# Attention and squared-ReLU block on one core: the turned pair of heads leaves for DRAM whole and returns in strips, and the opening loads x and w_proj in another order

## The reference, cut to what matters

```
xn  = layernorm(x)
qkv = xn @ Wqkv + bqkv                       # 16 heads of 32
attention over blocks of 128 tokens: a block sees itself and its two neighbours,
    masked to |kpos - qpos| <= 128, softmax(scores / sqrt(512))
a   = attn @ values, heads joined, @ Wout + bout
w(W)= ternary(W) * row scale                 # scale = mean |W| of a row
h   = xn @ w(w_fc).T + gate * (xn @ v.T @ fast_b.T @ u.T)
f   = max(h, 0)^2 @ w(w_proj).T
out = x + a + f
```

## Time and profile before

| | us |
|---|---|
| median of 3 runs | 2447.55 (2446.18 to 2448.85) |
| the profiled execution | 2450.27 |
| its span, first to last instruction | 2448.5 |
| TensorE busy | 2355.4 (96%) |
| VectorE busy | 1678.4 (69%) |
| ScalarE busy | 1378.8 (56%) |
| GpSimd busy | 440.5 (18%) |

### The profile page before, as it was taken

The page is one execution under the profiler, slowest core; times in us unless marked ns, Lnnn a source line. Parts: engine busy times, 40 slices in busy tenths (PEclk is TensorE's granted clock), DMA queues, the critical chain, the costliest instruction groups (busy, mean ns, idle before and its releaser), DMA issues.

```text
span 2448.5 us, 56233 instructions
## 1 busy us (share of the span) xinstructions
PE 2355.4 (96%) x19528; PEld 1919.7 (78%) x19528; DVE 1678.4 (69%) x4576; ACT 1378.8 (56%) x3488; POOL 440.5 (18%) x734
## 2 busy tenths in 40 slices
PE   6999999999999999988999999999999999999996
PEld 5788888888888888867787777777777878888785
DVE  5455545555554454436888888888888888888885
ACT  6333333333333333325777677777777777777774
POOL 2011111111111111002222222222222222222221
PEclk8999999999999999999999999999999999999998
DMA  4733344433334444315999999999999999999995
GB/s 158 218 110 106 104 119 120 120 107 107 111 105 118 120 120 120 94 43 160 267 291 278 272 287 281 288 280 288 283 280 287 290 278 287 290 290 283 287 279 174
DMA packets 437149, 495.74 MB, mean 202 GB/s; under 512 B 35728, under 2 KB 359824, under 8 KB 436416
## 3 DMA queue, kind: packets, MB, share of 16 engines
q1 hardware_dynamic: 436784, 492.71, 68.0%
q0 software_dynamic: 144, 0.17, 0.0%
HBM read 261.53 MB, written 231.21 MB: 201 GB/s over the span
## 4 chain that ended last, share of the span: by engine, by line
PE 13%; DMA 12%; ACT 9%; issue 7%; DVE 7%; SPq 6%; POOL 0%; POOLq 0%; DVEq 0%
ACT wqkv_raw L1124 6%; DMA wqkv_raw<-turned_blocks 5%; DMA pair_moved<-turned_pairs 5%; DVE wqkv_raw L1202 4%; PE job_ps L1503 4%; SPq L1015 3%; SPq L1007 3%; PE job_ps L1343 3%; PE score_ps L1430 3%; PE job_ps L1352 2%; ACT pT L1133 2%; DMA turned_pairs<-pair_blocks 1%; DVE pair_blocks L1229 1%; ACT k_hi L1152 1%; ACT q_hi L1149 1%
## 5 line engine op out<-in xcount | busy, mean ns | idle before, releaser
L1124 ACT ACTIVATE wqkv_raw<-wqkv_raw,neg_max 128x384 f32<-128x384 f32 (+1 forms) x1024 | 621.6, 608 | 223.1 <-DVE neg_max L1202 221.0
L637 ACT ACTIVATE relu<-up_ps,fc_scale 128x512 f32<-128x512 f32 x256 | 176.7, 690 | 632.7 <-PE up_ps L747 632.7
L1202 DVE CUSTOM_DVE_ANT_0 wqkv_raw<-score_ps,mask 128x384 f32<-128x384 f32 (+1 forms) x1024 | 504.1, 549 | 29.1 <-PE score_ps L1430 28.8
L698 DVE SCALAR_TENSOR_TENSOR sq<-up_ps,relu 128x512 f32<-128x512 f32 x256 | 177.2, 692 | 493.0 <-ACT relu L637 491.8
L757 PE MATMUL down_ps<-proj_T,sq_hi 128*128 128x512 f32 x1024 | 404.4, 395 | 1.5 <-DVE sq_lo L681 1.5
L759 PE MATMUL down_ps<-proj_T,sq_lo 128*128 128x512 f32 x1024 | 404.7, 395 | 0.0
L743 PE MATMUL up_ps<-f_xT_hi,fc_T 128*128 128x512 f32 x1024 | 399.4, 390 | 2.2 <-PEq L136 2.2
L745 PE MATMUL up_ps<-f_xT_lo,fc_T 128*128 128x512 f32 x1024 | 399.5, 390 | 0.0
L1219 DVE STREAM_TRANSPOSE wqkv_raw<-wqkv_raw 128x384 f32<-128x384 f32 (+1 forms) x508 | 283.5, 573 | 68.9 <-ACT wqkv_raw L1124 65.9
L1343 PE MATMUL job_ps<-xT_hi,wqkv_hi 128*128 128x256 f32 x1024 | 310.5, 303 | 0.1
L1343 PE MATMUL job_ps<-xT_lo,wqkv_hi 128*128 128x256 f32 x1024 | 289.5, 283 | 0.0
(11 more groups left out here) (158 smaller groups left out, 4391.2 us busy)
## 6 DMA issues: line engine op xcount, KB each, us to landing
turned_blocks<-wqkv_raw SPq DMA_DIRECT2D x123, 768.0 KB, 5.5
wqkv_raw<-turned_blocks SPq DMA_DIRECT2D x492, 192.0 KB, 3.9
turned_pairs<-pair_blocks SPq DMA_DIRECT2D x496, 96.0 KB, 2.7
pair_moved<-turned_pairs SPq DMA_DIRECT2D x124, 384.0 KB, 4.9
xT_hi<-xT SPq DMA_DIRECT2D x65, 256.0 KB, 5.8
xT_lo<-xT SPq DMA_DIRECT2D x65, 256.0 KB, 5.6
xT<-f_xT_hi SPq DMA_DIRECT2D x64, 256.0 KB, 2.9
xT<-f_xT_lo SPq DMA_DIRECT2D x64, 256.0 KB, 3.0
```

The source lines that it names most:

```text
L637: nc.scalar.activation(relu[:, s % 2, :], up_ps[:, s % 2, :], ACT.Relu, scale=fc_scale2[:, s:s + 1]).then_inc(relu_done, 1)
L698: nc.vector.scalar_tensor_tensor(sq[:, s % 2, :], up_ps[:, s % 2, :], 0.0, relu[:, s % 2, :], ALU.max, ALU.mult).then_inc(sq_done, 1)
L1124: nc.scalar.activation(probs[:, u, cols], probs[:, u, cols], ACT.Exp, bias=neg_max[:, u:u + 1], scale=-1.0, accum_out=prob_sum[:, u:u + 1] ...
L1202: nc.vector.tensor_tensor_reduce(out=probs[:, u, cols], in0=score_ps[:, h, cols], in1=mask[:, cols], scale=-SCORE_SCALE, scalar=3e38, op0= ...
```

## The change

The pair's transfers change shape. On the way out, the whole of `pair_blocks` goes in one transfer over 128 partitions; for the last token pair, where only two of three neighbours are seen, too. DRAM now holds it as [128 partitions][4 strips][3][64], so that a partition's part is one contiguous run of 3072 bytes where it was four of 768. On the way in, four transfers each fetch one strip into 32 partitions of `pair_moved`, as the blocks have done all along. The waits on `pair_out` and `pair_in` follow in number.

In the opening, the four blocks of x are issued one behind each of `w_fc` blocks 7 to 10, `w_proj` goes in halves of 512 KB: four of them behind `w_fc` blocks 12 to 15, four behind the last. VectorE does the low parts of x at its steps 16, 17, 18 and 19 in place of 14, 15, 17 and 18.

```diff
-        X_LOW_AT = (FB - 2, FB - 1, FB + 1, FB + 2)
+        X_LOW_AT = (FB, FB + 1, FB + 2, FB + 3)
...
+            def load_proj(piece):
+                k, half = divmod(piece, 2)
+                cols = slice(half * F // 2, (half + 1) * F // 2)
+                sp.dma_start(proj_rows[k][:, cols], w_proj[k * P:(k + 1) * P, cols]).then_inc(proj_here[k], 16)
...
-                if n == BUFS - 1:
-                    for b, here in enumerate(lead.x_here):
-                        sp.dma_start(lead.x_in[:, b, :], block_rows(x, b)).then_inc(here, 16)
-                if n >= FB - DC:
-                    k = n - FB + DC
-                    sp.dma_start(proj_rows[k], w_proj[k * P:(k + 1) * P, :]).then_inc(proj_here[k], 16)
+                if BUFS - 1 <= n < BUFS - 1 + DC:
+                    b = n - BUFS + 1
+                    sp.dma_start(lead.x_in[:, b, :], block_rows(x, b)).then_inc(lead.x_here[b], 16)
+                elif n >= FB - DC:
+                    load_proj(n - FB + DC)
+            for piece in range(DC, 2 * DC):
+                load_proj(piece)
...
-                for q in range(STRIPS):
-                    sp.dma_start(pair_dram[t % 2, q, :, :, 0:last, :].rearrange("a j w x -> j a (w x)"),
-                                 pair_blocks[q * DH:(q + 1) * DH, :, 0:last, :, :].rearrange("j a w h t -> j a (w h t)")
-                                 ).then_inc(pair_out, 16)
+                if last == 3:
+                    sp.dma_start(pair_dram[t % 2, :, :, :, :].rearrange("p a w x -> p (a w x)"),
+                                 pair_blocks.rearrange("p a w h t -> p (a w h t)")).then_inc(pair_out, 16)
...
-                sp.wait_ge(pair_out, 16 * STRIPS * (t + 1))
+                sp.wait_ge(pair_out, 16 * (t + 1))
                 if t >= 1:
                     sp.wait_ge(pv_done, t)
-                sp.dma_start(pair_moved[:, :, 0:last, :, :].rearrange("p q w h t -> p q (w h t)"),
-                             pair_dram[t % 2, :, :, :, 0:last, :].rearrange("q a j w x -> (a j) q (w x)")).then_inc(pair_in, 16)
+                for a in range(STRIPS):
+                    moved = pair_dram[t % 2, :, a, 0:last, :].rearrange("(q j) w x -> j q (w x)", j=DH)
+                    sp.dma_start(pair_moved[a * DH:(a + 1) * DH, :, 0:last, :, :].rearrange("j q w h t -> j q (w h t)"),
+                                 moved).then_inc(pair_in, 16)
...
-    pair_dram = nc.dram_tensor("turned_pairs", [2, P // DH, P // DH, DH, 3, 2 * DH], F32, kind="Internal").ap()
+    pair_dram = nc.dram_tensor("turned_pairs", [2, P, P // DH, 3, 2 * DH], F32, kind="Internal").ap()
```

More of the change, by code:

```diff
@@ L236, in sum_proj @@
             def sum_proj(n):
-                dve.wait_ge(proj_here[n], 16)
+                dve.wait_ge(proj_here[n], 32)
                 nc.vector.tensor_reduce(abs_sum[:, FB + n:FB + n + 1], rows(FB + n), AX_X, ALU.add,
@@ L402, in sum_abs @@
                 else:
-                    act.wait_ge(proj_here[n - FB], 16)
+                    act.wait_ge(proj_here[n - FB], 32)
                     w = proj_rows[n - FB]
@@ L1013, in move_pair_out @@
                 sp.wait_ge(pair_turned, MOVED * (t + 1))
-                for q in range(STRIPS):
-                    sp.dma_start(pair_dram[t % 2, q, :, :, 0:last, :].rearrange("a j w x -> j a (w x)"),
-                                 pair_blocks[q * DH:(q + 1) * DH, :, 0:last, :, :].rearrange("j a w h t -> j a (w h t)")
-                                 ).then_inc(pair_out, 16)
+                if last == 3:
+                    sp.dma_start(pair_dram[t % 2, :, :, :, :].rearrange("p a w x -> p (a w x)"),
+                                 pair_blocks.rearrange("p a w h t -> p (a w h t)")).then_inc(pair_out, 16)
+                else:
+                    sp.dma_start(pair_dram[t % 2, :, :, 0:last, :].rearrange("p a w x -> p a (w x)"),
+                                 pair_blocks[:, :, 0:last, :, :].rearrange("p a w h t -> p a (w h t)")).then_inc(pair_out, 16)
             def move_pair_in(t):
@@ L1227, in turn_pair @@
                 if h == 0 and t >= 1:
-                    dve.wait_ge(pair_out, 16 * STRIPS * t)
+                    dve.wait_ge(pair_out, 16 * t)
                 nc.vector.transpose(pair_blocks[:, :, seen.start:seen.stop, h, :].rearrange("p a w t -> p w a t"),
@@ L1487, in probs_times_values @@
                     if b == 1 and is_moved(t):
-                        pe.wait_ge(pair_in, 16 * (t + 1))
+                        pe.wait_ge(pair_in, 16 * STRIPS * (t + 1))
                     seen = blocks_seen(i, b)
```

## The result

| | before | changed |
|---|---|---|
| median, us (4 runs each) | 2446.86 (2444.58 to 2448.85) | 2404.36 (2401.08 to 2407.63) |
| the profiled execution, its span | 2450.27, 2448.5 | 2402.34, 2400.5 |
| start of the first up product | 59.42 | 52.22 |
| start of the first score product | 1124.66 | 1118.54 |
| mean step, 115 steps in mid attention | 10.207 | 9.935 |

The ratio is 0.9827, 95% interval 0.9808 to 0.9845: 42.5 us faster, where 38 were forecast. The two profiled executions differ by 47.9 us. Where these lie is seen from the value products that open the steps: the first one starts 6.2 us earlier (1133.3 against 1139.5), the eighth 11.0, the 123rd 42.3, the last 47.9. So in this pair of profiles the opening and the way into attention gave 6.2, the first seven steps 4.8, the 115 steps of the middle 31.3, and the last five 5.6.

A forecast was written before the change was run, and what follows sets the result against it. The prediction took TensorE's 9.79 us a step as attention's floor, with waits for data returning from DRAM above it. Attention -32.5 and opening -5.5 made -38 from 2447.55: 2409 us forecast, range 2394 to 2441.

The forecast's parts named there:

- Bound and floor: Attention: TensorE's floor is 9.79 us a step against a mean of 10.21; 0.42 us a step at most to gain.
- Fewer issues ahead of the blocks: Attention, SyncE: one pair-out issue for four lets the blocks' issues start up to 1.5 us earlier; 0.8 counted.
- So the long issue should leave the blocks: Attention, SyncE: with fewer transfers queued, the long issue moves off the blocks' strips; 0.65 us on average, bounds 0 and 1.3.
- The prediction's own sign of being wrong: Attention: block issues in fours still at 3 us would show that the queue's filling isn't the cause.
- Blocks' lead of 1.85 us: Attention: blocks come 0.8 + 0.65 + 0.4 = 1.85 us earlier, removing nearly all of 22.4 us of waits.
- Strips, +0.75 for the pair in: Attention: pair in as four strips at 220 GB/s takes 1.79 us instead of 1.04, so 0.75 us longer.
- 0.15 us a step left over: Attention: of 0.42 us a step, 0.15 stays for steps whose landings scatter by more than the lead; gain 0.27.
- SyncE finishing as before, 0.4 us of room: Attention: four pair-in issues leave SyncE as before, so the 0.4 us of room ahead of the next blocks' issue holds.
- Rival (3): Attention: a long issue on the last pair strip every step makes SyncE late; slower, 2497 us; chance 6%.
- Ends of the stage: Attention's ends: about 1.5 us gained in the first steps, no term for the last ones.
- Opening: Opening: low-rank products near 40.5 us, first up product near 54; 5.5 us gained, bounds 0 and 7.

The follow-up runs named there:

- e3: Changed kernel, but the pair goes out in one issue of 512 pieces of 768 bytes; 2412.34 us, ratio 0.9845 to the kernel before.
- e4: Changed kernel, but the pair goes out in four issues, together 128 pieces of 3072 bytes; 2446.26 us, ratio 0.9986 to the kernel before.
- e10: Changed kernel plus three tiny spare issues a step between the pair's way out and the blocks' way in; 2450.17 us, ratio 1.0011 to before.
- e11: Changed kernel plus three tiny spare issues a step behind the pair's way in; 2539.81 us, ratio 1.0380 to the kernel before.
- e9: Changed kernel plus 14 semaphore increments on SyncE in each attention step, ahead of its wait for the pair's squares; 2401.27 us in one profiled execution.
- e5: Changed kernel, but the pair goes out in four issues of 128 pieces of 768 bytes each; 2493.29 us, ratio 1.0187 to before.
- e8: The best version: changed kernel with strips of blocks and pair fetched in the order 0, 2, 1, 3; 2395.43 us, ratio 0.9787 to before.
- e2: Kernel before with the new opening alone, the pair's transfers as before; 2445.12 us, ratio 0.9978 to the kernel before.
- e6: Kernel before with only the opening's new order of loads; 2442.34 us in one profiled execution.
- e7: Kernel before with only the new VectorE steps for the low parts of x; 2444.59 us in one profiled execution.
- e1: Changed kernel with the opening of before, so the pair's new transfers alone; 2406.09 us, ratio 0.9827 to the kernel before.
- the ten profiles: Profiled executions of the changed kernel and nine follow-up kernels, all with the new opening; first up product at 52.22 to 55.68 us.

## Why the prediction was right

- **Bound and floor: right.** 9.79 us a step was taken from free steps; 55 of 115 steps now take no more than 9.80 (before 16), in the best version 92.
- **Fewer issues ahead of the blocks: right.** 0.8 us of 1.5 were counted; blocks in came 0.85 us earlier on average, and SyncE's wait for the blocks' landing took over as said. e3 shows that it isn't the pieces, and e4 and e10 that SyncE's issue time is enough to take all of it: three issues more cost 0.31 and 0.33 us a step, where the change had saved 0.27. In both, though, TensorE ends up waiting for the pair, since the four issues in stand behind as well; e11 against e10 shows that the place of an issue counts, 1.03 against 0.33.
- **"So the long issue should leave the blocks": this step failed.** The term was 0.65 us and was 0. Block fours over 2 us: 65 before, 63 after; long issues 206 and 200. The queue that has taken about eight transfers and lets one in as one lands was read from the opening's 0.47 and 0.80 us and from one long step; the issues' lengths neither follow the transfers in the queue (e3 and e4) nor SyncE's instructions (e9). On pair and blocks they come together with the transfers on the instruction queue q8. The prediction's own sign of being wrong, block fours still near 3 us, came true (43 of 112 over 2.5 us, before 54).
- **Blocks' lead of 1.85 us: mis-sized by that term and more.** Their landing moved from 8.86 to 7.99 us behind the pair's issue, 0.87. That sufficed, because the waits it had to remove summed to 22.4 us over 30 steps. The right total rests partly on that, and in this it was luck: a lead of half the forecast size removes nearly the same stall, and the 0.15 us left over had been put for scatter.
- **Strips, +0.75 for the pair in: right in form.** They land one after another over 1.67 us (1.8 forecast). Pair landed 0.56 us earlier within the step, 1.1 forecast. Their price on the time isn't known: with four issues out, one transfer in (before) makes 10.207 us and four (e4) 10.243, but e4 also sends larger pieces out, and with the small ones (e5) it is 10.570 at another layout of DRAM. One out and one in wasn't tried.
- **0.15 us a step left over: right in size, by an allowance,** 16.7/115 = 0.145, so -31.3 for 115 steps where -31.1 was forecast. It is not scatter that nothing helps, though: e8 takes two thirds of it.
- **"SyncE finishing as before, 0.4 us of room": wrong.** Behind the pair's issue SyncE finished at 5.27 us and now does at 6.25; the room was 1.06 us on average and is 0.17, in 72 of 112 steps none. The forecast read both from one step with a long issue, and let the long issue pay for the four issues in; it stayed, and SyncE's waits for the two landings grew (77.7 and 74.2 us from 1200 to 2330, before 13.9 and 26.4). Rival (3) was to begin at 6.3 us. That it didn't come was close. Its price was also added wrongly: 0.9 less 0.42 is 0.48, not 0.45.
- **Ends of the stage: mis-sized.** The first steps gave 4.8 us where 1.5 was put, the last five 5.6 where none was. The kernel before's profile is on the slow side there: by the means of four profiles with the old transfers (before, e2, e6, e7) and three with the new (changed, e1, e9) it is 3.6 and 3.8. On medians the total is 42.5, 4.5 beyond the forecast.
- **Opening: right.** Over the ten profiles the low-rank products start at 40.1 (40.5 forecast) and the first up product at 53.6 (54), 5.9 and 5.7 us earlier for 5.5 taken. w_fc's last block is taken at 23.45 in the changed kernel's profile (arrival 23.6 forecast), but at 24.9 on average over the ten, so that step was too early. In the pair of profiles the whole 7.2 us is still there at the feed-forward stage's last down product (1086.49 against 1093.70). The first value product has 6.2. The rest went at attention's first 32 products, behind an idle time of 8.85 us; in the changed kernel and then before:

```profile
1095.70:1101.70 6.00, 5.96 (x32) 1.31 (x33) 4.55 (x3) 6.00 (x4) 1.06 (x4) 0.59 0.92 292
```

```profile
1102.90:1107.80 4.90, 4.86 (x32) 1.15 (x32) 3.45 (x2) 4.90 (x3) 1.06 (x4) 0.72 0.83 278
```

The same 32 products take 1.1 us more where the granted clock was 0.59, nearer to the 1.2 GHz level, than where it was 0.72. TensorE did the same before both, 0.4 us of products in 9.2 us, so no row shows what makes the difference, and it isn't the new opening: e1, with the old one, needs 6.3 us from the first of these products to the next kind, before 4.9 and the changed kernel 6.0. The opening has such a place too. The first 3.8 us of up products have a granted clock of 0.57 in the changed kernel and 1.00 before, but 0.69 in e1 with the old opening and 1.00 in e9 with the new, and the lead of 7.2 us is whole again by the 100th up product.

## What to carry to other kernels

Where one queue starts every transfer, add up its issue time along the chain, and ask which issues stand ahead of the data that the bounding engine waits for; one in place of four there, with three more behind, was worth 1.7% here (e1) with the DMA engines at 94%. Then measure the room behind before putting anything there: three issues ahead cost 0.33 us a step, three behind 1.03. And check what a long issue hangs on before a term of a sum rests on it.

## What the runs showed of the hardware

- An issue on SyncE takes 0.30 to 0.34 us when the queue had been idle and 0.43 right behind another (medians, changed kernel); its shape can make it 0.52 or 0.60 (e3, e5). About one in seven takes over 0.7 us: the second of a step's two transfers of 256 KB nearly each time (105 of 114), and of the issues of pair and blocks 86 of 1150, with a transfer on the instruction queue q8 under way in 77 of these.
- A busy share of the DMA engines of 94 to 95% left room: 282 GB/s became 293 at 99% (1200 to 1800 us), and 295 at 95% with the strips in another order (1200 to 2330 us; the changed kernel has 292 at 98% there).
- Four strips of 32 partitions in the order 0, 2, 1, 3 land 0.2 us (blocks) and 0.4 us (pair) sooner after their first issue than in the order 0, 1, 2, 3.
